# Two-layer decoder on one core: input norms moved ahead of the bitnet weight scaling, score tiles preset on ScalarE, attention tables loaded from the sync queue

## The chip, the core and the metric

The kernel runs as one program on one core of a Trainium2 chip. The metric is the device time in microseconds from launch to end; lower is better. The engines are called as the profile calls them: PE (TensorE matmuls), PEld (its weight loads), DVE (VectorE), ACT (ScalarE), POOL (GpSimd) and SP (SyncE, which here only issues transfers).

## The reference, cut to what matters

Sixteen sequences of 128 tokens with 128 channels pass through two decoder layers, each with a self-attention part, a cross-attention part and a feed-forward part, and each part sits behind a plain layer norm. Only the pieces that the change touches are shown in code.

```python
x = x + _L0_attn_ref(_layernorm(x), ...)            # 4 encoder layers with linear attention
x = x + _L0_xattn_ref(_layernorm(x), ctx, ctx, mask, ...)
x = x + _L0_ffn_ref(_layernorm(x), w1, conv_w, conv_b, w2)   # bitnet layer
x = x + _L1_attn_ref(_layernorm(x), ...)            # top-64 attention
x = x + _L1_xattn_ref(_layernorm(x), ctx, ctx, ...) # channel attention
x = x + _L1_ffn_ref(_layernorm(x), Wg, Wu, Wd)      # 8 experts

# _L0_attn_ref begins:
x = math.sqrt(d) * x_in + _sinusoidal_pos_emb(t, d)[None]
h = _layernorm(x, ln1_s, ln1_b); q, k, v = h @ Wq + bq, h @ Wk + bk, h @ Wv + bv
# _L0_xattn_ref:
scores = jnp.where(mask == 0, NEG, q k^T / sqrt(8)); weights = softmax(scores)
# _L0_ffn_ref, for both weights:
def weight_quant(w):
    scale = 1.0 / jnp.clip(jnp.mean(jnp.abs(w)), 1e-05)
    return jnp.clip(jnp.round(w * scale), -1, 1) / scale
```

## The kernel before, in words

The sixteen sequences are cut into two halves of eight, and a half into two slots (s = 0, 1) of four sequences. A tile such as `xin[s]`, `h[s]` or `xs_of[half][s]` holds the four sequences of a slot, tokens on the partitions. The program is written out by hand for each engine; the order of the work is the order of that text, and semaphores join the engines.

The first half goes through the four encoder layers in a loop (`encode_half`, PE line 1708, DVE line 2386), then through cross attention and the bitnet feed-forward (`cross_and_forward(0)`). After that the second half's encoder steps are woven into the top-64 attention of the first half (`beside_encoder`, which is made of `merged_turn(b)` for b from -1 to 9), then `cross_and_forward(1)`, and then the rest of the top-64 attention with the experts.

The opening, ahead of the loop: POOL starts the load of the raw bitnet weights (`wc_raw`, which lies in the buffer `far0`), sets constant tiles, issues eight loads of attention tables on its own queue (lines 625 to 629) and then serves the norms. SP loads the two slots of x, then `ident`, `consts`, `pos`, `maskt`, `rowf` (semaphore `consts_in`, 80 when all five are in), and then the first layer's weights. DVE waits for `consts_in` at 80, quantizes the bitnet weights (lines 2215 to 2230: absolute sums, a cross-partition sum by one PE matmul at line 1704, scaling, rounding, clipping to `wcq`), and only then runs the norm of the inputs.

A layer norm of a slot is four `bn_stats` and four `bn_aggr` on DVE (lines 1878 and 1883), two small operations on POOL that make `rstd` (lines 637 and 639), and four `tensor_scalar` on DVE that write `h` (line 1890). The inputs are normed (LN_IN), scaled and given the position table (line 2247), and normed again (LN_A, the first norm of the encoder layer). PE transposes that `h` (line 1268), ACT copies it to `hT` (line 932), PE projects it (lines 1720 and 1722), and DVE adds the bias rows to keys and values (`kk`, `vv`, lines 2392 and 2393): the first `kk` is where the loop's steady work on DVE begins. These are counted in units of half a slot.

The masked scores of the cross attention are built by a predicated copy of PSUM into a tile `S` that must hold NEG beforehand. `S` has three buffers. POOL fills them with three memsets (`preset_scores`, line 828) twice: in the opening behind the first input norms, and in turn 9 of `beside_encoder`, behind the `rstd` of the cross-attention norm of the second half.

## Time and profile before

| | |
|---|---|
| three runs, median (lowest to highest) | 1449.4 us (1447.85 to 1454.92) |
| the profiled execution's own time | 1452.7 us |
| its span, first to last instruction | 1450.9 us |
| busy: PE, PEld, DVE, ACT, POOL | 1053.8, 695.7, 998.0, 671.1, 491.9 us |
| mean granted PE clock | 0.819 of full |

The busy times are sums over a program whose stages have different limits, so none of them says what bounds a given stage. The chain of work that ended last, followed back from the end, says which engine was waited for; the timeline of a stretch says what stood there. Both are in the rows further down. Times in a timeline count from the span's start.

### The profile page before, as it was taken

How to read it: one execution, taken by the hardware profiler on the slowest of the kernel's cores; microseconds unless marked ns; L12 is line 12 of the kernel's file. 1: busy time of each engine (PE TensorE's matmuls, PEld its weight loads, DVE VectorE, ACT ScalarE, POOL GpSimd, SP SyncE). 2: the span in 40 equal slices, each digit the busy share in tenths (PEclk: the TensorE clock that was granted, in tenths of full speed). 3: DMA queues.
4: the chain of work that ended last, by engine and by line, in shares of the span. 5: the costliest groups of instructions: out<-in, count | busy, mean ns of one | idle time of the engine just before them, and what ended most of it. 6: DMA issues, size and time to landing. Idle time of an engine off the chain costs nothing.

```text
span 1450.9 us, 17892 instructions
## 1 busy us (share of the span) xinstructions
PE 1053.8 (73%) x5079; PEld 695.7 (48%) x5082; DVE 998.0 (69%) x3100; ACT 671.1 (46%) x1767; POOL 491.9 (34%) x474
## 2 busy tenths in 40 slices
PE   2877775655476818777676669868899883888999
PEld 1766652323344515554454334433344462666887
DVE  5666657878637778778887886753776858765332
ACT  1443436733156526666423654325776653533322
POOL 5233235601335404444524730043343423331100
PEclk9898976765677767888655889989998986899999
DMA  3000110000000000000001001201111120223344
GB/s 124 21 18 29 29 41 9 1 0 1 0 10 21 12 3 17 14 17 9 1 1 51 1 1 37 66 22 47 52 45 45 48 73 15 67 77 92 113 135 123
DMA packets 41106, 53.88 MB, mean 37 GB/s; under 512 B 6112, under 2 KB 20080, under 8 KB 41008
## 3 DMA queue, kind: packets, MB, share of 16 engines
q1 hardware_dynamic: 40336, 50.80, 11.5%
q0 software_dynamic: 672, 1.98, 0.4%
q8 instruction: 37, 0.61, 0.2%
q14 instruction: 61, 0.50, 0.1%
HBM read 51.71 MB, written 1.05 MB: 36 GB/s over the span
## 4 chain that ended last, share of the span: by engine, by line
PE 49%; DVE 28%; ACT 7%; POOL 7%; issue 7%; DVEq 1%; DMA 0%; another core or an unknown queue 0%; SPq 0%; POOLq 0%; ACTq 0%
PE psum L1679 7%; PE psum L1690 6%; PE psum L1665 6%; PE psum L1450 2%; PE psum L1426 2%; PE psum L1757 2%; PE psum L1268 2%; PE psum L1346 2%; PE psum L1544 2%; DVE h L1890 2%; PE psum L1408 2%; PE psum L1764 2%; POOL Wk L680 2%; PE psum L1498 2%; ACT far L995 2%
## 5 line engine op out<-in xcount | busy, mean ns | idle before, releaser
L2188 DVE TENSOR_TENSOR big<-psum,qe 128x512 f32<-128x512 f32 x106 | 72.8, 687 | 154.7 <-PE psum L1690 75.4
L1144 ACT ACTIVATE qe<-psum 128x512 f32<-128x512 f32 x106 | 62.3, 596 | 124.4 <-PE psum L1679 120.3
L1665 PE MATMUL psum<-big,wexp 128*128 128x256 f32 (+1 forms) x340 | 115.8, 455 | 0.0
L995 ACT ACTIVATE far<-far,half_far,fmul 128x128 bf16<-128x128 bf16 x256 | 102.9, 488 | 22.7 <-DVE hit L1963 22.7
L637 POOL TENSOR_SCALAR veps<-mv 128x4 f32<-128x4 f32 x34 | 8.4, 246 | 294.6 <-DVE mv L1883 294.6
L1976 DVE MAX8 near<-Wk 128x8 f32<-128x128 f32 x512 | 103.0, 275 | 0.0
L1268 PE MATMUL psum<-ident,h 128*128 128x128 f32 x172 | 37.9, 347 | 78.4 <-DVE h L1890 53.3
L735 POOL TENSOR_TENSOR Wk<-Wk,far 128x1024 f32<-128x1024 f32 x32 | 68.2, 2136 | 67.9 <-ACT far L995 67.9
L1890 DVE TENSOR_SCALAR h<-xs,mv,rstd 128x128 f32<-128x128 f32 x128 | 57.9, 553 | 41.1 <-POOL rstd L639 37.9
L1665 PEld LDWEIGHTS psum<-big,wexp 128*128 128x128 f32 x340 | 69.0, 203 | 30.1 <-issue 21.9
L1346 PE MATMUL psum<-ident,Wk 128*128 128x128 f32 x256 | 48.0, 355 | 47.1 <-POOL Wk L680 44.2
L1690 PE MATMUL psum<-xin,wexp 128*128 128x512 f32 x128 | 70.4, 633 | 15.1 <-DVE far L2188 9.9
L973 ACT ACTIVATE S<-psum,tiny 128x1024 f32<-128x1024 f32 x32 | 35.7, 1114 | 92.3 <-PE psum L1408 92.3
L1679 PE MATMUL psum<-xin,wexp 128*128 128x512 f32 x128 | 76.0, 679 | 2.5 <-DVE vaug L2599 1.6
L985 ACT ACTIVATE far<-S 128x128 bf16<-128x128 f32 x256 | 75.0, 296 | 0.3
L726 POOL TENSOR_TENSOR Wk<-S,ngr 128x2048 f32<-128x2048 f32 x16 | 58.1, 3630 | 39.1 <-DVE hit L1963 39.1
L1346 PEld LDWEIGHTS psum<-ident,Wk 128*128 128x128 f32 x256 | 38.0, 182 | 69.0 <-POOL Wk L680 42.5
L1268 PEld LDWEIGHTS psum<-ident,h 128*128 128x128 f32 x172 | 23.5, 171 | 97.9 <-DVE h L1890 47.5
L757 POOL TENSOR_SCALAR nparts<-nmax 128x16 bf16<-128x16 f32 x16 | 5.2, 326 | 189.2 <-DVE nmax L2060 189.2
L1986 DVE MATCH_REPLACE8 Wk<-near,Wk 128x128 f32<-128x128 f32 x256 | 67.1, 273 | 0.0
L1426 PE MATMUL psum<-ctxT,kT 32*128 32x512 f32 x128 | 49.0, 848 | 23.4 <-DVEq L2054 22.2
L948 ACT ACTIVATE Wk<-S,nsm 128x128 f32<-128x128 f32 x128 | 49.5, 389 | 11.9 <-DVE nsm L2480 11.9
(343 smaller groups left out, 2915.0 us busy)
## 6 DMA issues: line engine op xcount, KB each, us to landing
wexp<-in_mg SPq DMA_DIRECT2D x48, 256.0 KB, 2.7
wexp<-in_mu SPq DMA_DIRECT2D x48, 256.0 KB, 3.0
wexp<-in_md SPq DMA_DIRECT2D x48, 256.0 KB, 3.0
w<-in_aw SPq DMA_DIRECT2D x8, 256.0 KB, 2.9
w<-in_w2a SPq DMA_DIRECT2D x8, 256.0 KB, 2.6
wqkv<-in_aw SPq DMA_DIRECT2D x8, 192.0 KB, 2.2
ctxt<-in_ctx SPq DMA_DIRECT2D x5, 256.0 KB, 4.6
xin<-in_x SPq DMA_DIRECT2D x4, 256.0 KB, 3.0
```

The lines of the kernel that those rows point to most:

```text
L735: pool.tensor_tensor(Wk[t][:, heads, :], Wk[t][:, heads, :], far[t][:, heads, :], ALU.subtract).then_inc(z_ready, 1)
L985: ins = act.activation(far[n % 2][:, hd, :], S[n % 3][:, hd, :], ACT.Sign, accum_out=cnt[n % 2][:, hd:hd + 1])
L995: ins = act.activation(far[t][:, hd, :], far[t][:, hd, :], ACT.Identity, bias=half_far[:, 0:1], scale=fmul[t][:, hd:hd + 1])
L1268: mm = pe.transpose(dst[:, b * P:(b + 1) * P], src[:, b, :], eye)
L1346: mm = pe.transpose(bank(4 + g % 2)[:, j * P:(j + 1) * P], E[a % 2][:, 4 * g + j, :], ident[:, :])
L1426: pe.matmul(bank(j), kT_of[g // 2][g % 2][rows, c * P:(c + 1) * P], qblk[a % 2][rows, :, :].rearrange("p i q -> p (i q)"), start=True, sto ...
L1665: mm = pe.matmul(bank(4)[:, 0:w], wd[l % 2][:, c + j, :], hid_of[k >= EARLY][k % CH][:, j * w:(j + 1) * w], start=first and j == 0, stop=l ...
L1679: mm = pe.matmul(bank(5 + k % 2)[:, j * w:(j + 1) * w], wg[l % 2][:, (c + j) * P:(c + j + 1) * P], hTm[g], start=True, stop=True)
L1690: mm = pe.matmul(bank(U_BANK[k])[:, j * w:(j + 1) * w], wu[l % 2][:, (c + j) * P:(c + j + 1) * P], hTm[g], start=True, stop=True)
L1890: ins = dve.tensor_scalar(h[s][:, b, :], src[:, b, :], mv[s][:, b, 0:1], rstd[s][:, b:b + 1], ALU.subtract, ALU.mult)
L1976: ins = dve.max(near[:, hd, rank:rank + 8], Wk[t][:, hd, :])
L2188: dve.tensor_tensor(hid_of[k >= EARLY][k % CH], bank(U_BANK[k]), sg_of[k >= EARLY][k % 2], ALU.mult).then_inc(hu_done, 1)
```

## The change

In words: DVE opens with the statistics of the inputs; the absolute sums of the bitnet weights are made on ACT (`Abs` with an accumulated output, its elementwise result thrown into `big0`); their scaling and rounding go in two pieces between and behind the norms of the first encoder layer. The score tiles are filled by ACT (Identity of a zero tile with NEG as bias) instead of POOL, in the opening as ACT's first work and in turns 8 and 9 of `beside_encoder`. The eight loads of attention tables and the loads of `maskt` and `rowf` go to the end of SP's opening list; `consts_in` is waited for at 48 (`ident`, `pos`, `consts`), and the attention tables' semaphore at 128 instead of 96. DVE waits once for all three presets. The first embedding is written out as `first_embedding`, with the two slots interleaved differently.

```diff
@@ SP, opening
-for dst, src in ((ident..), (consts..), (pos..), (maskt[:, :], mask)):
+for dst, src in ((ident..), (pos..), (consts..)):
     sp.dma_start(dst, src).then_inc(consts_in, 16)
-sp.dma_start(rowf[:, :], arow[L:L + 1, 0:2 * P].to_broadcast([P, 2 * P])).then_inc(consts_in, 16)
 for load in (load_qkv, load_out, load_up, load_down):
     load(0)
 for s in SL:
     load_ctx(s, s * G)
+sp.dma_start(maskt[:, :], mask).then_inc(attw_in, 16)
+sp.dma_start(rowf[:, :], ...).then_inc(attw_in, 16)
+for i in range(2):
+    sp.dma_start(watt[i]..), sp.dma_start(catt[i]..), sp.dma_start(ratt[i]..)   # attw_in
+sp.dma_start(rowe..), sp.dma_start(cole..)                                      # ew_in
@@ POOL
+pool.memset(masked[:, :], NEG)
-for i in range(2):
-    pool.dma_start(watt[i]..), pool.dma_start(catt[i]..), pool.dma_start(ratt[i]..)
-pool.dma_start(rowe..), pool.dma_start(cole..)
 pool.wait_ge(preset, 1)
-pool.wait_ge(consts_in, 80)
 for s in SL:
     ln_rsqrt(s, LN_IN)
+pool.wait_ge(consts_in, 48)
-def preset_scores():
-    for t in range(3):
-        pool.memset(S[t][:, :, :], NEG).then_inc(s_preset, 1)
@@ POOL, beside_encoder, turn NB + 1
-    pool.wait_ge(drop_done, NB)
-    preset_scores()
@@ POOL, ahead of encode_half
-preset_scores()
@@ ACT
+def preset_scores(t):
+    act.activation(S[t][:, :, :], zeros[:, :].unsqueeze(1).to_broadcast([P, H, P]), ACT.Identity, bias=masked[:, 0:1]).then_inc(s_preset, 1)
 act.wait_ge(preset, 1)
+for t in range(3):
+    preset_scores(t)
+act.wait_ge(cw_in, 32)
+for k in range(2):
+    act.activation(big[0][:, k, :], wc_raw[:, k, :], ACT.Abs, accum_out=wsum[:, k:k + 1]).then_inc(wq_sem, 1)
@@ ACT, beside_encoder
 for b in range(-1, NB + 2):
+    if b == NB + 1:
+        act.wait_ge(drop_done, NB)
+        preset_scores((NB - 1) % 3)
     merged_turn(b)
...
     if b == NB:
         beside(4)
+        for n in (NB - 3, NB - 2):
+            act.wait_ge(drop_done, n + 1)
+            preset_scores(n % 3)
         context_keys(1)
@@ PE
-pe.wait_ge(consts_in, 80)
+pe.wait_ge(consts_in, 48)
@@ DVE
-dve.wait_ge(consts_in, 80)
-dve.wait_ge(preset, 1)
-dve.tensor_copy(identb..); dve.tensor_scalar(neg_big..)
-dve.wait_ge(cw_in, 32)
-for k in range(2):
-    dve.tensor_reduce(wsum[:, k:k + 1], wc_raw[:, k, :], AX.X, ALU.add, apply_absolute_value=True).then_inc(wq_sem, 1)
-...                       # wscale, wrs, scaling, rounding, clipping
 for s in SL:
     dve.wait_ge(x_in[s], 16)
     layer_norm(s, LN_IN, xin[s])
-for s in SL:
-    normalize(s, LN_IN, xin[s])
+def first_embedding():
+    def embedded(s):
+        normalize(s, LN_IN, xin[s])
+        if s == 0:
+            dve.wait_ge(consts_in, 48)
+        dve.wait_ge(ln_h, both(s, LN_IN + 1))
+        dve.scalar_tensor_tensor(xs_of[0][s].., h[s].., float(np.sqrt(P)), pos.., ALU.mult, ALU.add).then_inc(x_upd, 2)
+    embedded(0)
+    dve.wait_ge(x_upd, both(0, LN_A))
+    layer_norm(0, LN_A)
+    embedded(1)
+    normalize(0, LN_A)
+    dve.wait_ge(x_upd, both(1, LN_A))
+    layer_norm(1, LN_A)
+    weights_scaled()      # waits for the PE sum; wscale, wrs, scaling of both weights
+    normalize(1, LN_A)
+    weights_rounded()     # rounding, identb, neg_big, clipping to wcq
@@ DVE, cross_and_forward
-if b < 3:
-    dve.wait_ge(s_preset, hf * 3 + (b + 1))
+if b == 0:
+    dve.wait_ge(s_preset, hf * 3 + 3)
```

DVE's first instructions in the program before, from behind two small operations on `ident` up to the first norm written to `h`, read as follows (`xs0_0` is the first half's slot 0 of x, `far0` holds the raw bitnet weights).

```order
L2219 TENSOR_REDUCE wsum<-far0 128x1 x2
L2221 TENSOR_SCALAR wscale<-psum 128x2
L2223 RECIPROCAL wrs<-wscale 128x2
L2226 TENSOR_SCALAR far0<-far0,wrs 128x512 x2
L2228 TENSOR_SCALAR far0<-far0 128x1024
L2230 TENSOR_SCALAR wcq<-far0 128x1024
L1878 BN_STATS stats0<-xin0 128x6 x4
L1883 BN_AGGR mv0<-stats0 128x2 x4
L1878 BN_STATS stats1<-xin1 128x6 x4
L1883 BN_AGGR mv1<-stats1 128x2 x4
L1890 TENSOR_SCALAR h0<-xin0,mv0,rstd0 128x128 x4
L1890 TENSOR_SCALAR h1<-xin1,mv1,rstd1 128x128 x4
```

The same engine in the changed program, from the second slot's embedding to the entry of the encoder loop; the four statistics groups of the inputs, slot 0's first `h`, its embedding and its second statistics stand ahead of these rows.

```order
L2253 SCALAR_TENSOR_TENSOR xs0_1<-h1,pos 128x512
L1901 TENSOR_SCALAR h0<-xs0_0,mv0,rstd0 128x128 x4
L1889 BN_STATS stats1<-xs0_1 128x6 x4
L1894 BN_AGGR mv1<-stats1 128x2 x4
L2230 TENSOR_SCALAR wscale<-psum 128x2
L2232 RECIPROCAL wrs<-wscale 128x2
L2235 TENSOR_SCALAR far0<-far0,wrs 128x512 x2
L1901 TENSOR_SCALAR h1<-xs0_1,mv1,rstd1 128x128 x4
L2239 TENSOR_SCALAR far0<-far0 128x1024
L2240 CAST identb<-ident 128x128
L2241 TENSOR_SCALAR neg_big<-ident 128x128
L2243 TENSOR_SCALAR wcq<-far0 128x1024
```

The weight work moved from ahead of the first norm to both sides of the last one, and the two reductions that made `wsum` are gone from this engine.

On ACT, between turn 8 and turn 9 of `beside_encoder`, the program before has these rows (`at`, `kT1` and `hT` carry the cross attention's context, keys and queries of the second half; line 1004 is the softmax exponential of the top-64 attention).

```order
L1135 ACTIVATE se2<-se2 128x256
L1197 COPY at0<-psum 128x512
L1197 COPY at1<-psum 128x512
L1200 ACTIVATE kT1_0<-psum,catt0 128x512
L1200 ACTIVATE kT1_1<-psum,catt0 128x512
L1004 ACTIVATE wexp<-psum 128x1024
L927 COPY hT0<-psum 128x512
```

The changed program has there:

```order
L1138 ACTIVATE se2<-se2 128x256
L1156 ACTIVATE S2<-zeros,masked 128x2048
L1156 ACTIVATE S0<-zeros,masked 128x2048
L1209 COPY at0<-psum 128x512
L1209 COPY at1<-psum 128x512
L1212 ACTIVATE kT1_0<-psum,catt0 128x512
L1212 ACTIVATE kT1_1<-psum,catt0 128x512
L1156 ACTIVATE S1<-zeros,masked 128x2048
L1001 ACTIVATE wexp<-psum 128x1024
L924 COPY hT0<-psum 128x512
```

Two presets stand ahead of the copies of the context, and the third between the keys and the exponential.

## Rows read from the trace of the kernel before

**Rows 1.** The page's chain that ended last, by engine.

```profile
PE 49%; DVE 28%; ACT 7%; POOL 7%; issue 7%; DVEq 1%; DMA 0%; another core or an unknown queue 0%; SPq 0%; POOLq 0%; ACTq 0%
```

**Rows 2.** The chain's pieces in the opening: start us, us, what.

```profile
1.24 0.49 SPq L483
...
2.79 0.43 SPq L534
...
3.74 4.89 DMA rowf<-in_arow
```

**Rows 3.** DMA issues of the opening: size, median us from issue to landing.

```profile
xin<-in_x SPq DMA_DIRECT2D x1, 256.0 KB, 4.5
...
pos<-in_pos SPq DMA_DIRECT2D x1, 64.0 KB, 4.4
```

**Rows 4.** Timeline of DVE in the opening: start us, us, engine, line.

```profile
8.66 0.23 DVE L2215 CAST identb<-ident 128x128 bf16<-128x128 f32 x1 [8.66 <-DMA rowf<-in_arow]
...
10.95 0.16 DVE L2221 TENSOR_SCALAR wscale<-psum 128x2 f32<-128x2 f32 x1 [0.74 <-PE psum L1704]
...
12.26 0.69 DVE L2228 TENSOR_SCALAR far<-far 128x1024 f32<-128x1024 f32 x1
...
13.60 0.87 DVE L1878 BATCH_NORM_STATS2 stats<-xin 128x6 f32<-128x128 f32 x4
...
16.76 1.12 DVE L1890 TENSOR_SCALAR h<-xin,mv,rstd 128x128 f32<-128x128 f32 x4 [0.49 <-POOL rstd L639]
...
18.10 5.86 DVE L1890 TENSOR_SCALAR h<-xin,mv,rstd 128x128 f32<-128x128 f32 x4 [0.23 <-POOL rstd L639]
...
23.88 0.68 DVE L2247 SCALAR_TENSOR_TENSOR xs<-h,pos 128x512 f32<-128x512 f32 x1
...
25.62 0.38 DVE L1883 BATCH_NORM_AGGREGATE mv<-stats 128x2 f32<-128x6 f32 x4
...
27.66 1.11 DVE L1890 TENSOR_SCALAR h<-xs,mv,rstd 128x128 f32<-128x128 f32 x4 [1.67 <-POOL rstd L639]
...
33.77 0.42 DVE L2392 TENSOR_TENSOR kk<-psum,rowkv 128x256 f32<-128x256 f32 x1
```

**Rows 5.** POOL: its last constant tile, and line 828, all instructions.

```profile
4.03 0.22 POOL L623 MEMSET zeros<- 128x128 bf16 x1
...
L828 POOL MEMSET S<- x6: 1805/1806/1807, 18.0 to 762.5; 128x2048 f32 x6
```

**Rows 6.** Timeline of PE in the opening.

```profile
28.32 1.20 PE L1268 MATMUL psum<-ident,h 128*128 128x128 f32 x4 [17.41 <-DVE h L1890]
...
35.15 1.13 PE L1720 MATMUL psum<-wqkv,hT 128*128 128x256 f32 x4 [0.80 <-ACT hT L932]
```

**Rows 7.** ACT instruction groups by form: busy us, mean ns of one, idle before.

```profile
L985 ACT ACTIVATE far<-S 128x128 bf16<-128x128 f32 x256 | 75.0, 296 | 0.3
...
L951 ACT ACTIVATE Wk<-S 128x1024 f32<-128x1024 f32 x16 | 16.7, 1043 | 0.0
...
L1044 ACT ACTIVATE ke<-kk 128x512 f32<-128x512 f32 x8 | 5.0, 628 | 0.0
```

**Rows 8.** Timelines of DVE, PE and ACT around turn 9.

```profile
747.52 0.59 ACT L1197 COPY at<-psum 128x512 f32<-128x512 f32 x1 [8.72 <-PE psum L1268]
...
757.44 1.02 ACT L1004 ACTIVATE wexp<-psum 128x1024 f32<-128x1024 f32 x1 [3.81 <-PE psum L1433]
...
759.11 5.86 DVE L1890 TENSOR_SCALAR h<-xs,mv,rstd 128x128 f32<-128x128 f32 x4 [0.69 <-POOL rstd L639]
...
764.58 1.03 PE L1433 MATMUL psum<-neg_big,drop 128*128 128x128 bf16 x8
...
767.64 1.26 DVE L2440 TENSOR_TENSOR vv<-psum,ratt 128x512 f32<-128x512 f32 x2
...
768.40 1.08 PE L1268 MATMUL psum<-ident,h 128*128 128x128 f32 x4 [2.79 <-issue]
```

**Rows 9.** PE by windows: stretch, its us, busy (count), granted clock, DMA.

```profile
760.00:780.00 20.00, 15.36 (x58) 0.50 0.00 1
...
0.00:1450.00 1450.00, 1053.75 (x5079) 0.82 0.12 37
```

More of the change, by code:

```diff
@@ L321, in decoder @@
         tiny = sb("tiny", [P, 1])
+        masked = sb("masked", [P, 1])
         neg_big = sb("neg_big", [P, P], BF16)
@@ L532, in _ @@
                 load_x(s, s * G)
-            for dst, src in ((ident[:, :], ident_d), (consts[:, :], const_d), (pos[:, :], pos_d), (maskt[:, :], mask)):
+            for dst, src in ((ident[:, :], ident_d), (pos[:, :], pos_d), (consts[:, :], const_d)):
                 sp.dma_start(dst, src).then_inc(consts_in, 16)
-            sp.dma_start(rowf[:, :], arow[L:L + 1, 0:2 * P].to_broadcast([P, 2 * P])).then_inc(consts_in, 16)
             for load in (load_qkv, load_out, load_up, load_down):
@@ L539, in _ @@
                 load_ctx(s, s * G)
+            sp.dma_start(maskt[:, :], mask).then_inc(attw_in, 16)
+            sp.dma_start(rowf[:, :], arow[L:L + 1, 0:2 * P].to_broadcast([P, 2 * P])).then_inc(attw_in, 16)
+            for i in range(2):
+                sp.dma_start(watt[i][:, :], (bw, dw)[i]).then_inc(attw_in, 16)
+                sp.dma_start(catt[i][:, :], (bcol, dcol)[i]).then_inc(attw_in, 16)
+                sp.dma_start(ratt[i][:, :], (brow, drow)[i].to_broadcast([P, 2 * P])).then_inc(attw_in, 16)
+            sp.dma_start(rowe[:, :, :].rearrange("p a c -> p (a c)"), erow.to_broadcast([P, 10 * P])).then_inc(ew_in, 16)
+            sp.dma_start(cole[:, :], ecol).then_inc(ew_in, 16)
             for hf in range(1):
@@ L2210, in act_scales @@
                 dve.tensor_scalar(asc[s][:, :], asc[s][:, :], 127.0, None, ALU.mult).then_inc(c_step[s], 1)
-            dve.wait_ge(consts_in, 80)
-            dve.wait_ge(preset, 1)
-            dve.tensor_copy(identb[:, :], ident[:, :])
-            dve.tensor_scalar(neg_big[:, :], ident[:, :], -BIG, None, ALU.mult)
-            dve.wait_ge(cw_in, 32)
-            for k in range(2):
-                dve.tensor_reduce(wsum[:, k:k + 1], wc_raw[:, k, :], AX.X, ALU.add, apply_absolute_value=True).then_inc(wq_sem, 1)
-            dve.wait_ge(wsum_mm, 1)
-            dve.tensor_scalar(wscale[:, :], bank(7)[:, 0:2], 1.0 / (P * FH), 1e-5, ALU.mult, ALU.max).then_inc(wq_sem, 1)
-            dve.wait_ge(wq_sem, 3)
-            dve.reciprocal(wrs[:, :], wscale[:, :]).then_inc(wq_sem, 1)
-            dve.wait_ge(wq_sem, 4)
-            for k in range(2):
-                dve.tensor_scalar(wc_raw[:, k, :], wc_raw[:, k, :], wrs[:, k:k + 1], MAGIC, ALU.mult, ALU.add).then_inc(wq_sem, 1)
-            dve.wait_ge(wq_sem, 6)
-            dve.tensor_scalar(wc_raw[:, :, :], wc_raw[:, :, :], MAGIC, 1.0, ALU.subtract, ALU.min).then_inc(wq_sem, 1)
-            dve.wait_ge(wq_sem, 7)
-            dve.tensor_scalar(wcq[:, :, :], wc_raw[:, :, :], -1.0, None, ALU.max).then_inc(wq_sem, 1)
             for s in SL:
@@ L2235, in _, with weights_scaled, weights_rounded @@
                 layer_norm(s, LN_IN, xin[s])
-            for s in SL:
-                normalize(s, LN_IN, xin[s])
+            def weights_scaled():
+                dve.wait_ge(wsum_mm, 1)
+                dve.tensor_scalar(wscale[:, :], bank(7)[:, 0:2], 1.0 / (P * FH), 1e-5, ALU.mult, ALU.max).then_inc(wq_sem, 1)
+                dve.wait_ge(wq_sem, 3)
+                dve.reciprocal(wrs[:, :], wscale[:, :]).then_inc(wq_sem, 1)
+                dve.wait_ge(wq_sem, 4)
+                for k in range(2):
+                    dve.tensor_scalar(wc_raw[:, k, :], wc_raw[:, k, :], wrs[:, k:k + 1], MAGIC, ALU.mult, ALU.add).then_inc(wq_sem, 1)
+            def weights_rounded():
+                dve.wait_ge(wq_sem, 6)
+                dve.tensor_scalar(wc_raw[:, :, :], wc_raw[:, :, :], MAGIC, 1.0, ALU.subtract, ALU.min).then_inc(wq_sem, 1)
+                dve.tensor_copy(identb[:, :], ident[:, :])
+                dve.tensor_scalar(neg_big[:, :], ident[:, :], -BIG, None, ALU.mult)
+                dve.wait_ge(wq_sem, 7)
+                dve.tensor_scalar(wcq[:, :, :], wc_raw[:, :, :], -1.0, None, ALU.max).then_inc(wq_sem, 1)
+            def first_embedding():
[4 more added lines that the diff above has]
+                    dve.wait_ge(ln_h, both(s, LN_IN + 1))
+                    dve.scalar_tensor_tensor(xs_of[0][s][:, :, :], h[s][:, :, :], float(np.sqrt(P)), pos[:, :].unsqueeze(1).to_broadcast([P, G, P]),
+                                             ALU.mult, ALU.add).then_inc(x_upd, 2)
+                embedded(0)
[8 more added lines that the diff above has]
+                weights_rounded()
             def embed(hf):
@@ L2612, in cross_and_forward @@
                         normalize(s, n0 + (NLN + LN_IN), xin[s])
-            embed(0)
+            first_embedding()
             encode_half()
```

13 lines of the change are left out of this document (4 added, 9 removed).

## The prediction, made before the changed kernel ran

> **What bounds the kernel now.** I read the page's chain that ended last first. PE holds 49% of it and DVE 28% [rows 1]: no single engine bounds the program, so a saving counts only where the chain passes. The change touches two places, the opening and turn 9 of the interleaved encoder, so I read the chain and the timelines of these two.
>
> In the opening PE stands still until 28.32 us, for 17.41 us of it waiting for `h` from DVE [rows 6]. DVE is the engine that everybody waits for. It does nothing until 8.66 us, when the last of the five constant loads, `rowf`, has landed: the chain has a piece of 4.89 us for that transfer [rows 2, 4]. Then it works on the bitnet weights until 13.60, when the statistics of the inputs begin [rows 4]. The inputs had been there long before: the second slot of x was issued at 1.24 and took 4.5 us, so it lay ready at 5.74 [rows 2, 3].
>
> There is a third loss in the same stretch. Four `tensor_scalar` of one norm take 1.12 us at 16.76, but the next four, the same instruction on the other slot, take 5.86 us at 18.10 [rows 4]. They lie beside POOL's three memsets of the score tiles, of 1.806 us each, the first of which starts at 18.0 [rows 5]. The same picture returns near 759: four such instructions take 5.86 us while the other three of the six memsets run, whose last starts at 762.5 [rows 5, 8].
>
> **The opening, step by step.** What is new is DVE's order. I price each step from its own row and let it start when the one before it ends or its input is there. A statistics pass (stats and aggregate) is the time from the end of the embedding (23.88 + 0.68 = 24.56) to the end of the aggregates (25.62 + 0.38 = 26.00), so 1.44 us; from there to the norm that uses it, through POOL's two small operations, it is 27.66 - 26.00 = 1.66 us [rows 4].
>
> Slot 1 of x lands at 5.74; its pass ends at 7.2, slot 0's having run before it. Norm of slot 0, 1.12: 8.3. Embedding, 0.68: 9.0; it needs `pos`, which landed at 2.79 + 4.4 = 7.2 even with more transfers ahead [rows 2, 3]. Pass of slot 0, 1.44: 10.4. Norm and embedding of slot 1, 1.12 + 0.68: 12.2. Norm of slot 0 for the encoder, whose `rstd` is there at 10.4 + 1.66 = 12.1, 1.11: 13.4. Pass of slot 1: 14.8. Scaling of the weights, from 10.95 to 12.26 in the old timeline, 1.31: 16.1. Norm of slot 1, `rstd` there at 14.8 + 1.66 = 16.5, 1.11: 17.6. Rounding and clipping, 13.60 - 12.26 = 1.34, and two casts of at most 0.23 each: 19.4. So the first `kk` comes at 19.4 instead of 33.77 [rows 4]: **14.4 us earlier**. Of these, 5.86 - 1.12 = 4.7 are the memsets' share.
>
> What lies beside it. PE must first do the little sum of the weights, and that now waits for ACT: three presets and two Abs passes behind POOL's last constant tile, which ends at 4.03 + 0.22 = 4.25 [rows 5]. A preset of 2048 elements is an operation that the trace does not show. The nearest row is the longest plain SBUF-to-SBUF activation, 1043 ns for 1024 elements; against 628 ns for 512 that is 0.81 ns an element, so 1.04 + 0.83 = 1.87 us, and at most 2.09 as two of them [rows 7]. The far upper bound is sixteen instructions of 128 elements, 16 x 296 ns = 4.7 us; the lower bound is that of an operation hidden altogether, zero [rows 7]. I take 2.0, since this one has a bias column and one instruction pays its start only once. ACT is then through at 4.25 + 6.0 = 10.3. The Abs passes are 128x512, 0.63 each and something for the accumulated output, 1.5 together: 11.8. PE has the sum well before 13, and DVE asks for it at 14.8. It costs nothing; the slack is about 2.5 us, or 0.8 a preset.
>
> The Trainium skill, "ScalarE: Activation LUTs", section "What ACT_TABLE_LOAD costs", gives an activation with a bias column as about 1990 ns at 2048 elements, with 93 ns of overlap between neighbours. By it three presets take 5.8 us and the sum stays the same; no row of the trace before has such an instruction.
>
> PE's own work fits too. In the old order the third unit's projections are done at 35.15 + 1.13 = 36.28, 2.5 us after the second `h` was complete and `kk` began at 33.77 [rows 4, 6]. From 17.6 that gives 20.1, and DVE reaches the third unit only some 2.5 us behind its first `kk`, at 21.9. So DVE's weight rounding is what is late next, by 1.8 us, and that is in the sum.
>
> The loads. SP's first three transfers keep their places, the layer weights move two issues forward, and the eight table loads leave POOL's queue for the end of SP's. They feed the cross attention, which comes after all four encoder layers of the first half: cost nothing. If SP's queue were slow in taking them, the next layer's weights would wait behind them; but these are only asked for when the first layer's attention is done. POOL loses eight issues that nobody waited for.
>
> **Turn 9.** Without the memsets the four `tensor_scalar` at 759.11 take 1.1 us, so DVE is 4.7 us earlier from there. PE does not follow by as much. It finished its batch at 764.58 + 1.03 = 765.61 and then stood 2.79 us until 768.40 [rows 8], although the `h` it transposes was ready at 764.97. In the code it also waits for the first `vv` of the cross values (`pv_done`), whose pair of instructions began at 767.64, so the first ended at 768.3 [rows 8]. With DVE 4.7 us earlier that is 763.6, before PE is free at 765.61. So the whole gap goes: **2.8 us**, and PE's own batch is next.
>
> On ACT the presets of `S2` and `S0` (4 us) fall in the 8.72 us in which it stood idle ahead of 747.52, and that of `S1` in the 3.81 us ahead of 757.44 [rows 8]. If that cover were gone the third would delay the exponential by 2.0 us.
>
> **Sum.** 14.4 + 2.8 = 17.2 us. The profiled execution took 1452.7, which gives 1435.5; the median of the three runs is 1449.4, 3.3 below it, and gives 1432. I forecast **1432 us**.
>
> **The rivals.**
> *Only the opening pays.* At turn 9 another wait replaces the removed one, or the gain meets work further on that is not earlier (the experts' loads, a POOL step). For it: DVE moves 4.7 and PE only 2.8, so there are joints at which gains shrink. Against it: PE is on the chain there, and what it does next is its own. 1449.4 - 14.4 = 1435. Chance 0.14.
> *The presets are slow.* If an activation that reads a repeated zero tile goes at the short instructions' rate, 4.7 us each [rows 7], ACT has the absolute sums at 4.25 + 14.2 + 1.5 = 20.0. PE cannot transpose before 20.6; DVE, at 14.8, waits for the sum until 20.6, and `kk` comes at 20.6 + 1.3 + 1.1 + 1.8 = 24.8. Gain 9 in the opening, 11.8 in all: 1438. It decides from 2.8 us a preset on. Chance 0.07.
> *The clock rises.* Around turn 9 PE has 0.50 of its clock, the 1.2 GHz level, with 15.36 us of work in 20 [rows 9]. A closed gap there could bring the upper level sooner; half of 15.36 is 7.7, and if two thirds of it are on the path, 5 us more are gained: 1427. The Trainium skill, "TensorE: Matmul & The Clock Gate", section "HAM oscillation — how this bites in real kernels", says that idle gaps of PE bring the lower clock; no row says yet that this gap does. Chance 0.08.
> *The clock takes part back.* Every later stage starts some 15 us earlier against whatever else sets the clock, and stretches at 0.50 may fall elsewhere. 6 us back: 1438. Chance 0.07.
> *Slower than before, by the clock.* PE's part of the chain is 0.49 x 1450.9 = 711 us at a mean of 0.82 [rows 1, 9]. To lose the 17.2 and 7.2 more, 711 x (0.82 / c - 1) must be 24.4, so c = 0.793. Above 1456.6 from there on. Against it: no engine gets more idle time. Chance 0.03; with c between 0.80 and 0.81 the result is no change, 1442 to 1456, with other absorptions 0.05.
>
> **How the numbers follow.** The forecast, both gains to within 5 us, has the remaining 0.56. Its bounds, the rival with the opening alone, the slow presets and the clock either way lie between 1426 and 1440; that holds a little over 0.8. What a measurement here tells from no change is 0.5%, 7.2 us. Faster by more than that, below 1442.2: 0.92. Within it: 0.05. Slower: 0.03.
>
> **What would show it.** In the changed trace: DVE's first statistics before 6 us instead of at 13.60; the four `tensor_scalar` of both norms at 1.1 us; ACT's presets at 2.0 us each and the absolute sums by 12; PE's first transposes near 13; the first `kk` near 19.4; around turn 9 no 5.86 us group, and no gap of 2.8 us ahead of PE's second set of transposes. Wrong would be: `tensor_scalar` still at 5.86 (another partner than the memsets), a transfer that lands later than x or `pos` did, the sum of the weights later than 15 us, or a mean clock that differs by 0.01 or more, which alone is worth 9 us.

## The result and the profile after

| | before | after |
|---|---|---|
| median of the executions (us) | 1450.77 (1447.85 to 1454.92, 4 runs) | 1432.62 (1430.56 to 1438.47, 4 runs) |
| ratio, 95% interval | | 0.9882 (0.9847 to 0.9917) |
| profiled execution, its span (us) | 1452.7, 1450.9 | 1434.47, 1432.3 |
| its mean granted clock | 0.819 | 0.822 |

The change makes the kernel 18 us faster. The forecast was 1432, in a range of 1426 to 1440. The same kernel, timed again with others (again_after below), gave 1430.94 against 1453.09, ratio 0.9873 (0.9831 to 0.9915). One execution of weights_late below took 1582.62 us at a mean granted clock of 0.667, and is left out of its figures.

The chain that ended last, from the page of after, answers to [rows 1]; its pieces in the opening answer to [rows 2] (start us, us, what):

```profile
PE 49%; DVE 28%; ACT 8%; issue 7%; POOL 6%; DVEq 1%; DMA 0%; another core or an unknown queue 0%; SPq 0%; POOLq 0%; ACTq 0%
```

```profile
2.32 0.43 SPq L535
...
2.79 5.45 DMA consts<-in_const
```

The chain still begins with a load, but it is that of `consts`, and it holds the embedding up for only 0.17 us, as DVE's timeline of after says (to be held against [rows 4]):

```profile
3.57 0.87 DVE L1889 BATCH_NORM_STATS2 stats<-xin 128x6 f32<-128x128 f32 x4 [3.57 <-DMA xin<-in_x]
...
7.09 1.09 DVE L1901 TENSOR_SCALAR h<-xin,mv,rstd 128x128 f32<-128x128 f32 x4
8.34 0.69 DVE L2253 SCALAR_TENSOR_TENSOR xs<-h,pos 128x512 f32<-128x512 f32 x1 [0.17 <-DMA consts<-in_const]
...
14.89 0.88 DVE L2235 TENSOR_SCALAR far<-far,wrs 128x512 f32<-128x512 f32 x2
...
16.31 1.12 DVE L1901 TENSOR_SCALAR h<-xs,mv,rstd 128x128 f32<-128x128 f32 x4 [0.53 <-POOL rstd L641]
...
18.82 0.42 DVE L2421 TENSOR_TENSOR kk<-psum,rowkv 128x256 f32<-128x256 f32 x1
```

ACT in the opening, then the group of all presets, which is the row that [rows 7] did not have (count: shortest/middle/longest ns):

```profile
4.32 5.79 ACT L1156 ACTIVATE S<-zeros,masked 128x2048 f32<-128x2048 bf16 x3 [2.30 <-POOL zeros L632]
...
11.15 0.19 ACT L1163 ACTIVATION_READ_ACCUMULATOR big<-far 128x1 f32 x1
```

```profile
L1156 ACT ACTIVATE S<-zeros,masked x6: 1986/1991/2001, 4.3 to 735.6; 128x2048 f32<-128x2048 bf16 x6
```

PE in the opening, against [rows 6]:

```profile
12.85 1.20 PE L1280 MATMUL psum<-ident,h 128*128 128x128 f32 x4 [0.82 <-DVE h L1901]
...
20.19 1.13 PE L1731 MATMUL psum<-wqkv,hT 128*128 128x256 f32 x4 [1.17 <-ACT hT L929]
```

The timelines of DVE, PE and ACT of after around turn 9, against [rows 8]:

```profile
720.79 3.88 ACT L1156 ACTIVATE S<-zeros,masked 128x2048 f32<-128x2048 bf16 x2
...
735.62 1.99 ACT L1156 ACTIVATE S<-zeros,masked 128x2048 f32<-128x2048 bf16 x1
...
740.87 1.12 DVE L1901 TENSOR_SCALAR h<-xs,mv,rstd 128x128 f32<-128x128 f32 x4 [0.69 <-POOL rstd L641]
...
740.33 0.63 PE L1280 MATMUL psum<-ident,h 128*128 128x128 f32 x4 [0.83 <-DVE h L1901]
...
744.02 0.62 PE L1445 MATMUL psum<-neg_big,drop 128*128 128x128 bf16 x8
745.42 0.63 PE L1280 MATMUL psum<-ident,h 128*128 128x128 f32 x4 [0.77 <-issue]
746.78 1.13 PE L1295 MATMUL psum<-hT,watt 128*128 128x512 f32 x2 [0.73 <-ACT hT L924]
747.74 3.69 PE L1462 MATMUL psum<-vaug,wexp 128*128 128x10 f32 x32
```

Everything on the list of what would show the forecast right is there: DVE's first statistics at 3.57, none of the norms' `tensor_scalar` groups in the opening and in turn 9 longer than 1.12, presets of 1.99 us, sums through by 11.34, PE's first transposes at 12.85, the first `kk` at 18.82. At turn 9 PE stands 0.77 us instead of 2.79. But something else moved there too. Eight matmuls on `neg_big` take 0.62 us instead of 1.03 [rows 8]. In the kernel before, the first transposes and the two groups behind the second ones are these:

```profile
758.57 0.84 PE L1268 MATMUL psum<-ident,h 128*128 128x128 f32 x4 [1.16 <-DVE h L1890]
...
770.22 2.08 PE L1283 MATMUL psum<-hT,watt 128*128 128x512 f32 x2 [0.73 <-ACT hT L927]
772.08 6.84 PE L1450 MATMUL psum<-vaug,wexp 128*128 128x10 f32 x32
```

They take 0.63, 1.13 and 3.69 us after. That is the upper level of the clock, 2.4 GHz, instead of the lower one, 1.2 GHz.

PE's matmuls come in the same order in all of these kernels. So the start of the k-th matmul in two traces can be subtracted, and each stretch shows what it gains or gives back. Most traces hold 5,079 matmuls; those of presets_only, t9_pool, open_pool and tables_pool hold three more, whose records the others lack, and the table counts without these three. The table is worked out from the traces: the time of the k-th matmul in the first trace of before, then how much earlier (-) it starts in the other traces.

```
matmul  before |  again_  again_  |  after  again_ | presets_  t9_    open_ | xb_
                  before  before_2          after      only    pool   pool  | late
   14     32.5    -0.1     +0.6    -15.0   -14.9      -3.6    -15.0  -11.5   -15.1
  900    254.8    -0.1     -1.8    -14.7   -17.0      -8.0    -17.1  -14.4   -27.6
 1050    297.6    -0.1     -4.7    -17.5   -19.9      -7.6    -19.9  -14.4   -27.6
 2550    755.5    -0.1     -5.2    -17.9   -20.4      -6.7    -20.3  -14.4   -24.3
 2640    785.4    -0.1     -5.2    -27.4   -29.8      -9.7    -21.4  -24.0   -33.9
 3300    987.5    -0.1     -5.2    -24.9   -27.3     -10.1    -20.3  -24.6   -34.5
 3600   1097.3    -0.2     -5.2    -21.2   -23.7     -10.1    -16.8  -21.1   -31.0
 4500   1326.9    -0.1     -5.2    -18.5   -23.7      -7.4    -15.3  -17.9   -28.1
  end   1447.9    -0.1     -5.2    -18.7   -23.7      -7.5    -13.6  -17.9   -28.4
```

In the column of after, the opening brings 15.0 and keeps it (14.7 at 254.8). Another 2.7 come between 254.8 and 297.6. Turn 9 brings 9.5, and from there to 1326.9 some 9 are given back. PE by windows shows whose gain and loss that is (stretch, its us, PE busy and count, granted clock, DMA). The stretches are set so that nearly the same matmuls lie in them, first in before and then in after:

```profile
755.00:785.00 30.00, 22.84 (x95) 0.56 0.03 7
812.00:903.00 91.00, 65.20 (x286) 0.88 0.05 15
903.00:1097.00 194.00, 163.42 (x601) 0.91 0.14 43
```

```profile
737.00:758.00 21.00, 16.10 (x98) 0.84 0.07 19
784.00:877.00 93.00, 69.18 (x282) 0.82 0.05 15
877.00:1076.00 199.00, 167.90 (x603) 0.90 0.13 42
```

The same work keeps PE busy for 6.7 us less in the first stretch, and for 4.0 and 4.5 us more in the other two. The granted clock is higher in the first and lower in the others.

### The profile page after: what moved, and what is told of

The parts are those of the page before. It is cut to its first block, busy times and chain, and to the rows that moved or that the text cites. A ratio compares the mean times of both kernels' runs of the same rounds, so it can differ in the third digit from the quotient of the medians.

```text
span 1432.3 us, 17890 instructions
## 1 busy us (share of the span) xinstructions
PE 1051.4 (73%) x5079; PEld 694.3 (48%) x5082; DVE 987.0 (69%) x3098; ACT 679.6 (47%) x1774; POOL 477.7 (33%) x461
## 4 chain that ended last, share of the span: by engine, by line
PE 49%; DVE 28%; ACT 8%; issue 7%; POOL 6%; DVEq 1%; DMA 0%; another core or an unknown queue 0%; SPq 0%; POOLq 0%; ACTq 0%
PE psum L1691 7%; PE psum L1702 6%; PE psum L1677 6%; PE psum L1768 2%; PE psum L1438 2%; PE psum L1462 2%; PE psum L1280 2%; PE psum L1556 2%; PE psum L1420 2%; PE psum L1775 2%; DVE h L1901 2%; PE psum L1358 2%; PE psum L1510 2%; POOL Wk L682 2%; ACT far L992 2%
## 5 line engine op out<-in xcount | busy, mean ns | idle before, releaser
L1901 DVE TENSOR_SCALAR h<-xs,mv,rstd 128x128 f32<-128x128 f32 x128 | 53.1, 477 | 38.4 <-POOL rstd L641 35.1
```

Source lines behind the costliest of these rows:

```text
L1901: ins = dve.tensor_scalar(h[s][:, b, :], src[:, b, :], mv[s][:, b, 0:1], rstd[s][:, b:b + 1], ALU.subtract, ALU.mult)
```

## The experiments

**t9_pool: turn 9 undone alone.** The opening stays as changed. POOL presets the tiles at turn 9, and ACT's presets there are taken out.

```diff
+            def preset_scores():
+                for t in range(3):
+                    pool.memset(S[t][:, :, :], NEG).then_inc(s_preset, 1)
...
                     if b == NB + 1:
+                        pool.wait_ge(drop_done, NB)
+                        preset_scores()
...
```

> The changed kernel with the three presets of turn 9 back on POOL as memsets; the opening as changed. Theory A (the memsets hold up DVE, and PE waits for DVE there): the four tensor_scalar beside them take 5.9 us again, and PE's second set of transposes in turn 9 comes 2.8 us later than in the changed kernel at the low clock, up to 4.7 us at the high one, where PE waits less on itself. Time 3 to 5 us over the changed kernel. Rival B (what the changed kernel gained there came from the clock alone, which rose at turn 9): tensor_scalar slow, but PE's later start of the scores is the same within 1 us when the clock is the same, and the time is the changed kernel's within 1 us.

Measured: 1440.26 (1437.81 to 1443.35, 6 runs), ratio 0.9911 (0.9886 to 0.9936) to a before of 1453.62. DVE's, POOL's and PE's timelines at turn 9:

```profile
738.36 5.29 POOL L832 MEMSET S<- 128x2048 f32 x3
...
738.44 5.86 DVE L1901 TENSOR_SCALAR h<-xs,mv,rstd 128x128 f32<-128x128 f32 x4 [0.68 <-POOL rstd L641]
...
737.90 0.63 PE L1280 MATMUL psum<-ident,h 128*128 128x128 f32 x4 [0.83 <-DVE h L1901]
...
747.73 1.09 PE L1280 MATMUL psum<-ident,h 128*128 128x128 f32 x4 [5.52 <-DVE vv L2469]
749.55 2.08 PE L1295 MATMUL psum<-hT,watt 128*128 128x512 f32 x2 [0.73 <-ACT hT L930]
```

PE stands 5.5 us, and behind that its matmuls are at the lower level again. In the table the kernel is level with again_after up to matmul 2550 and 8.4 us behind it at 2640. So taking the memsets out of turn 9 is worth 8 us here, more than the 3 to 5 expected; the wait makes 5.52 - 0.77 = 4.7 of it, and the slower matmuls the rest.

The first transposes, ahead of that wait, are still at the upper level (0.63 us, behind a stand of 0.83). So it wasn't the closed gap that kept the clock up there: the kernel before has the lower level at this place, and so has presets_only. The stand ahead of the first transposes is 0.83 to 0.85 us in all ten traces with the new opening, and 1.14 to 1.17 in the three of before and that of presets_only. The third of a microsecond comes from DVE, which begins the group of instructions ahead of it sooner, in before and then in after:

```profile
750.23 0.69 DVE L2444 TENSOR_TENSOR h<-h,rowf 128x512 f32<-128x512 f32 x1 [1.41 <-issue]
```

```profile
732.00 0.69 DVE L2473 TENSOR_TENSOR h<-h,rowf 128x512 f32<-128x512 f32 x1 [1.08 <-issue]
```

"issue" is time in which DVE waited for nothing that the profile shows. It is 1.41 in the four traces with the old opening and 1.08 to 1.09 in the ten with the new one. No experiment moved it alone, so that it tips the clock is argued, not shown.

**open_pool: the opening's memsets undone alone.** POOL presets the tiles behind the two input norms.

```diff
...
+            preset_scores()
             encode_half()
...
             act.wait_ge(preset, 1)
-            for t in range(3):
-                preset_scores(t)
```

> The changed kernel with the opening's presets back on POOL as memsets behind the rstd of the inputs; ACT does only the absolute sums there. Theory A: the memsets fill POOL from 8.9 to 14.2 us. DVE's norm of slot 1 at 10.4 is held until about 14.2, and the rstd of the first encoder norm, asked for at 10.5, comes only at 15.5 instead of 12.2. First kk at 22.5 instead of 18.8, time 3.5 to 4 us over the changed kernel. Rival B (order of DVE alone made the gain, the memsets cost nothing): first kk within 0.5 us of 18.8.

Measured: 1433.12 (1429.85 to 1434.86, 5 runs), ratio 0.9851 (0.9824 to 0.9878). The first `kk` comes at 22.20, 3.4 us later, because one norm meets the memsets:

```profile
10.49 4.36 DVE L1904 TENSOR_SCALAR h<-xin,mv,rstd 128x128 f32<-128x128 f32 x4
```

The local step is as expected, and the time is not: it can't be told from that of after.

**tables_pool: the table loads back on POOL.** The eight transfers of attention tables are issued by POOL ahead of its first norm; the rest stays as changed.

```diff
             pool.memset(zeros[:, :], 0.0).then_inc(preset, 1)
+            for i in range(2):
+                pool.dma_start(watt[i][:, :], (bw, dw)[i]).then_inc(attw_in, 16)
+                pool.dma_start(catt[i][:, :], (bcol, dcol)[i]).then_inc(attw_in, 16)
+                pool.dma_start(ratt[i][:, :], (brow, drow)[i].to_broadcast([P, 2 * P])).then_inc(attw_in, 16)
...
```

> The changed kernel with the eight loads of attention tables issued by POOL again, behind its constant tiles, as in the kernel before; maskt and rowf stay at the end of SP's list. The prediction held that nobody waited for these issues. Theory A (true only in the old order): eight issues of 0.52 us keep POOL from 4.3 until 8.5 us, so the rstd of the inputs' slot 0 is ready at 9.8 instead of 6.6, DVE's first norm starts at 9.8 instead of 7.1 and the first kk comes at 21.5, 2.7 us later; time 2 to 3 us over the changed kernel. Rival B (the prediction's own reading, nobody waits): first kk within 0.3 us of 18.8, time the same.

Measured: 1433.21 (1431.59 to 1435.85, 4 runs), ratio 0.9857 (0.9825 to 0.9889). POOL begins its two small operations only at 8.54, when its last issue is done, and DVE waits:

```profile
7.89 0.53 POOL L632 DMA_DIRECT2D cole<-in_ecol  x1
...
9.95 1.12 DVE L1901 TENSOR_SCALAR h<-xin,mv,rstd 128x128 f32<-128x128 f32 x4 [2.90 <-POOL rstd L641]
```

The first `kk` comes at 21.68, 2.9 us later than after. Moving the loads is a part of the opening's gain, then. The time again doesn't show it. By the traces both kernels are still 3.2 to 3.5 us behind the trace of after at matmul 150 (65 us) and within 0.4 of it at 750 (196 us). But they are 2.3 to 2.6 behind again_after there, so this catching up is no larger than the scatter between two executions of one kernel. Whether the 3 us are paid up to turn 9 stays open. Behind it something else covers them: both traces of after lose 2.5 to 2.6 us between 2640 and 3300, and open_pool and tables_pool gain 0.6 there.

**presets_only: ACT's presets alone, in the old order.**

```diff
...
-            preset_scores()
             encode_half()
...
             act.wait_ge(preset, 1)
+            for t in range(3):
+                preset_scores(t)
...
```

> The kernel before with nothing changed but the presets: all six on ACT, in the opening and in turns 8 and 9. Theory A: both groups of tensor_scalar at 1.1 us instead of 5.9; first kk at 29.0 instead of 33.8; PE's transposes in turn 9 another 2.8 us earlier or more. Time 7 to 9 us under the kernel before, so the order of the opening is worth the other 10. Rival B (in the old order the removed stall is filled by the next wait, POOL's rstd): first kk not before 31, time 3 to 5 us under the kernel before.

Measured: 1445.19 (1440.62 to 1445.92, 6 runs), ratio 0.9931 (0.9905 to 0.9957): 8.4 us less than before. The first `kk` comes at 29.96, 3.8 us earlier; it would be 4.7, but `rowf` landed at 9.60 instead of 8.66. At turn 9, where ACT has the presets too, the table gives 3.0 us, close to the predicted 2.8. PE's timeline there:

```profile
751.86 0.84 PE L1275 MATMUL psum<-ident,h 128*128 128x128 f32 x4 [1.17 <-DVE h L1897]
...
757.88 1.03 PE L1440 MATMUL psum<-neg_big,drop 128*128 128x128 bf16 x8
758.70 1.06 PE L1275 MATMUL psum<-ident,h 128*128 128x128 f32 x4
```

The gap ahead of the second transposes is gone whole, yet PE had come to the lower level at 751.86, with the first transposes, after 1.17 us of idling, and stays there. So this kernel shows the step by itself, without the clock's share.

**again_after and again_before: how much is scatter.** Both are unaltered kernels.

> The changed kernel again, unaltered, timed beside the three below on one chip, so that they can be compared with it and not with a kernel before that ran elsewhere. Theory A (each local step is worth its time, the granted clock adds or takes a few us): 1432 to 1436 us, so that open_pool (1433.1) and tables_pool (1433.2) are level with it although their first kk is 2.8 to 3.3 us later. Theory B (those two lost their 3 us on the path all the way and only ran on a chip or at a moment that favoured them): this one comes out near 1430 us, ratio to before 0.983 or lower. The profile should show the first kk again within 0.5 us of 18.8, the second transposes of turn 9 without a gap of more than 1 us, and the matmuls behind them at 1.1 us for four.

> The kernel before, unaltered, for a second trace of it, to see how far two executions of one kernel part by the granted clock alone. Theory A (the 8 us that the changed kernel gave back between 900 and 1330 us are scatter of the clock: the first trace of before had the clock at 0.91 there by chance): this trace's clock over 1000 to 1200 us is nearer 0.85 to 0.88, and its matmuls there are 3 us or more later against the first trace. Theory B (they belong to the change: the experts run slower when what is ahead of them ended sooner): the clock there is 0.90 or more again and the two traces agree within 2 us at every matmul. Turn 9: PE's second transposes again 2.8 us after the first, and the matmuls behind them at 2.1 us for four.

> The kernel before a third time, as again_before: by theory A the clock over 1000 to 1200 us scatters between traces by 0.02 or more, by theory B the three agree within 0.01.

Measured: again_after 1430.94 (1426.31 to 1440.81, 6 runs), its profiled execution 1429.46; the two of before 1452.68 and 1447.53. In the table, again_before agrees with the first trace to 0.2 us at every matmul. again_before_2 runs 5.2 us ahead, and has all of that by 432 us; 2.9 of them fall between 254.8 and 297.6, where after gained its 2.7. From there on all three are parallel; their clock from 1000 to 1200 us is 0.91, 0.91 and 0.90. So the 2.7 us are scatter. What was given back behind turn 9 is so only for the smaller part. Up to matmul 3600 both traces of after give back the same 6.1 to 6.2 us, and no trace of before does. Of these, 3.6 fall between 3300 and 3600, in all ten traces with the new opening; the other 2.5 to 2.6 fall before 3300, in both traces of after and in joints_late, but not in open_pool, tables_pool, weights_late and xb_late. The further 2.7 up to 4500 are in the first trace of after and not in again_after; ten of the eleven traces of changed kernels lose 1.5 to 3.5 us there. Theory A of these expectations falls for the larger part, and holds at most for these 2.7.

**xb_late: another meeting of POOL and DVE taken away.** POOL's two additions of the attention's output bias wait for the last unit's queries.

```diff
                     pool.wait_ge(wo_in, i * 32 + 32)
+                    pool.wait_ge(q_pos, nth_unit(UNITS - 1, i + 1))
                     for s in SL:
                         pool.tensor_tensor(xb[s][:, :, :], xs[s][:, :, :], bc(rowo[:, :]), ALU.add).then_inc(xbo_done, 1)
```

> In every layer GpSimd's tensor_tensor adds of the bias row wait until the last unit's normalised input has been written, instead of running beside VectorE's residual adds; nothing else changes. In the changed kernel these residual adds of VectorE take 1.47 and 1.49 us beside GpSimd and 0.53 and 0.41 us elsewhere. Theory A (an elementwise GpSimd instruction holds up a VectorE instruction that meets it): the two groups fall to about 0.5 and 0.4 us, some 2 us a layer, 4 layers, so 6 to 8 us less: 1425 to 1428 us against 1433 of the changed kernel. Rival (the VectorE adds are slow for another reason, a PSUM read for example): the groups stay at 1.5 us and the time at 1433. Second rival (they fall, but PE's clock takes the gain back): groups at 0.5 us and 1430 to 1433 us.

(The two DVE groups form the positive keys and queries; to call them residual additions was a slip of the expectation.) Measured: 1419.99 (1418.5 to 1424.69, 5 runs), ratio 0.9779 (0.9745 to 0.9814), 11 us below again_after in the same comparison. It beats both kernels. The first layer in after, then in xb_late:

```profile
24.32 2.72 POOL L883 TENSOR_TENSOR xb<-xs,rowo 128x512 f32<-128x512 f32 x2
...
24.46 1.47 DVE L1909 SCALAR_TENSOR_TENSOR big<-ke,big 128x256 f32<-128x256 f32 x1
25.85 1.49 DVE L1914 SCALAR_TENSOR_TENSOR qT<-qe,qT 128x256 f32<-128x256 f32 x1
```

```profile
24.14 0.42 DVE L1910 SCALAR_TENSOR_TENSOR big<-ke,big 128x256 f32<-128x256 f32 x1
24.49 0.42 DVE L1915 SCALAR_TENSOR_TENSOR qT<-qe,qT 128x256 f32<-128x256 f32 x1
...
25.25 0.41 DVE L2433 TENSOR_TENSOR kvs<-psum,consts 128x256 f32<-128x256 f32 x1
...
25.06 2.50 POOL L884 TENSOR_TENSOR xb<-xs,rowo 128x512 f32<-128x512 f32 x2 [1.02 <-DVE qT L1915]
```

Theory A holds at the rows, 1.47 + 1.49 - 0.42 - 0.42 = 2.1 us a layer and 8.5 in four; POOL's additions start 0.7 us later and hold up nobody. In the table the lead over again_after is 10.6 us at 254.8; the 2 above the sum I put down to the clock, and by the end of the two profiled executions 4.7 remain. The profiled one of xb_late was the slowest of its five. The medians say 11, more than the 6 to 8 expected.

**joints_late: and one more, at the joint to the cross attention.** On top of xb_late, POOL spreads the first two rows before it makes the second slot's `rstd`, and the third row and the bias additions come behind that.

```diff
-                for b in range(2):
-                    spread(b)
+                spread(0)
+                spread(1)
                 if hf == 0:
+                    ln_rsqrt(1, LN_B)
                     pool.wait_ge(attw_in, 16 * 8)
+                spread(2)
...
-                spread(2)
...
```

> xb_late, and in addition at the joint of self and cross attention GpSimd first gives the 1/std of the first two units and only then spreads the third row; the bias adds come behind it. In the changed kernel one VectorE normalisation at 199.1 us takes 4.50 us beside GpSimd's tensor_tensor adds, where its like take 1.1. Theory A: that instruction comes down to 1.1 to 1.5 us and the copy of the following scores at 204.1 us comes about 1.8 us earlier, so 1 to 2 us below xb_late. Rival (the gain goes into the wait for the score copy on ScalarE): the instruction falls but the score copy stays at 204, and the time is that of xb_late within 0.5 us.

Measured: 1420.72 (1413.21 to 1433.97, 6 runs), ratio 0.9785 (0.9738 to 0.9832). The norm came down from 4.50 to 1.11 us, but the norm of the other slot, which now meets the two spreads, went up from 1.11 to 2.57, and PE makes DVE wait 1.16 us behind it. So the copy of the first scores came from 191.27 to 190.16, 1.1 us. The time can't be told from xb_late's.

**weights_late: is the weight rounding late next?** Scaling and rounding move behind the self attention, to an idle stretch of DVE ahead of their first use.

```diff
+                    if hf == 0 and b == 3:
+                        weights_rounded()
...
-                weights_rounded()
```

> The scaling and rounding of the ternary weights moves from in front of the first kk to a place behind the last unit's statistics, where VectorE idles 6.3 us. The prediction said that the rounding would be late next, by 1.8 us, once the norms open the program. Theory A: the first kk comes at 16.4 to 17.5 instead of 18.8 us, but the third unit's matmuls wait for ScalarE's copy of their transposes, so only 0.5 us or so reaches the third kk (21.4) and the time is 1432 to 1433.5, the same as the changed kernel within the measurement. Rival (all of the rounding was on the path): the third kk at 19 us and the time about 2.4 us lower. Slower by 1 to 3 us if the moved work lands in front of something that waits for VectorE.

Measured: 1432.44 (1429.85 to 1434.71, 5 runs), ratio 0.9863 (0.9828 to 0.9898), which can't be told from again_after. The first `kk` is at 17.01 instead of 18.66, the third only at 20.85 instead of 21.21, since DVE now waits 0.81 us for PE's third unit:

```profile
20.85 0.42 DVE L2420 TENSOR_TENSOR kk<-psum,rowkv 128x256 f32<-128x256 f32 x1 [0.81 <-PE psum L1731]
```

**memset_waits and memset_pieces: how the hold works.** Both start from t9_pool. One waits for the end of each memset; the other cuts each in four.

```diff
                     pool.memset(S[t][:, :, :], NEG).then_inc(s_preset, 1)
+                    pool.wait_ge(s_preset, 3 + t + 1)
```

```diff
-                    pool.memset(S[t][:, :, :], NEG).then_inc(s_preset, 1)
+                    for g in range(0, H, 4):
+                        ins = pool.memset(S[t][:, g:g + 4, :], NEG)
+                    ins.then_inc(s_preset, 1)
```

> t9_pool again (all three score tiles preset by GpSimd at turn 9), with GpSimd waiting for the completion of each memset before it issues the next. In t9_pool one VectorE tensor_scalar that met the three memsets at 738.4 took 5.86 us, about their whole 5.29 us. Theory A (VectorE is shut out as long as GpSimd's memsets follow without a break, and gets in at a break): the instruction takes 2 to 2.6 us, and PE's second transposes come some 3 to 3.7 us after where they were in t9_pool's own order, near 744 rather than 747.7. Rival (the instruction's four parts each lose to a memset whatever lies between, or VectorE's access is slowed all the time while GpSimd has any memset left): it stays above 5 us.

> t9_pool again with each of the three memsets cut into four (twelve of 128x512 in a row, no wait between them). Theory A (the hold lasts as long as the memsets follow without a break, whatever their size): the VectorE tensor_scalar that meets them stays at 5 to 6 us. Rival (it lasts one memset, and t9_pool's long one was only unlucky in meeting three of its parts): it takes under 3.5 us, since a memset now takes about 0.5 us. The time of this kernel is near t9_pool's 1440 us by the first, near 1436 by the second, which one look can't settle; the row decides.

Measured: 1442.74 and 1443.73, one execution each. The four instructions of the norm by themselves, with the waits, and then with the pieces:

```profile
L1902 DVE TENSOR_SCALAR h<-xs,mv,rstd x4: 1609/1760/1900, 741.8 to 743.9; 128x128 f32<-128x128 f32 x4
```

```profile
L1903 DVE TENSOR_SCALAR h<-xs,mv,rstd x4: 329/2894/5646, 743.1 to 749.0; 128x128 f32<-128x128 f32 x4
```

In t9_pool the same line reads:

```profile
L1901 DVE TENSOR_SCALAR h<-xs,mv,rstd x4: 327/2712/5285, 738.4 to 744.0; 128x128 f32<-128x128 f32 x4
```

With twelve short memsets in a row (524 to 525 ns each) the group took 6.22 us, and its first instruction 5.646. So the length of a memset doesn't matter, the unbroken row does: the rival of memset_pieces falls. With breaks the hold ends at each, but two of the four instructions get in and the next two meet the next memset: 3.76 us, neither the 2 to 2.6 of theory A nor the over 5 of the rival. Theory A had the mechanism, and counted one memset too few. PE stood 3.46 us instead of 5.52 ahead of the second transposes, and was at the lower level behind that too.

## Why the prediction was right

**The opening, 14.4 us.** Measured at the first `kk`, 33.77 - 18.82 = 14.95; on PE, 15.0, of which 14.7 are still there at 255 us. Down to the scaling of the weights, through at 14.89 + 0.88 = 15.77 instead of 16.1, every step lies within 0.4 us of its forecast, and the rounding overlapped a little more than priced.

**"Of these, 4.7 are the memsets' share."** Right as a mechanism. In the old order their removal gave 3.8 (0.9 lost to a later `rowf`); in the new order their return costs 3.4, since a norm met only 4.36 us of them.

**The preset, 2.0 us.** Measured 1.99. Here the Trainium skill, "ScalarE: Activation LUTs", section "What ACT_TABLE_LOAD costs", with its 1990 ns, was nearer than the reach from neighbouring rows (1.87); this trace agrees with it.

**"Weight rounding is late next, by 1.8 us."** This step failed, without harm to the sum. It looked at when DVE reaches the third unit and took PE's projections as done at 20.1. They began at 20.19, after 1.17 us of waiting for ACT's copy, and ended at 21.32; the third `kk` began at 21.36. weights_late showed it: 1.65 us at the first `kk` and 0.36 at the third.

**"POOL loses eight issues that nobody waited for."** Right in the old order and wrong in the new one: tables_pool puts 2.90 us of DVE's wait there. I had priced the removal in an order in which the norms came late. In the sum this did no harm either, since the sum was built on the new order with the loads gone.

**Turn 9, 2.8 us.** presets_only has it alone: 3.0. In the changed kernel turn 9 brought 9.5. The rest is the rival *the clock rises*, which I gave 0.08 and 5 us: PE stayed at the upper level from its first transposes until 751 us, and its matmuls there took about half their time. The rival had the mechanism only in part. It let the closed gap of 2.79 us bring the level; the level was there before that gap, with the new opening and its shorter stand of 0.83 us, and the closed gap kept it. The opening alone gains 1.1 us at turn 9 (t9_pool, where the wait swallows the rest), the presets alone 3.0 (presets_only), both together 9.5. All of open_pool, tables_pool, again_after and weights_late have both, and 9.5 to 9.6 us.

**The clock takes part back** had 0.07 and 6 us, and it happened too: some 9 us between 785 and 1327. The rows of one place, before and after, for the same matmuls:

```profile
1055.99 1.02 PE L1665 MATMUL psum<-big,wexp 128*128 128x512 f32 x2
```

```profile
1031.81 1.91 PE L1677 MATMUL psum<-big,wexp 128*128 128x512 f32 x2
```

There is no wait in it. Between matmuls 3300 and 3600 all ten traces with the new opening lose 3.6 us, and presets_only and the three traces of before lose none. The first 0.3 of it come before the clock differs. DVE aggregates a norm without a break in before, and with one in after:

```profile
991.18 0.38 DVE L2113 BATCH_NORM_AGGREGATE mv<-stats 128x2 f32<-128x6 f32 x4
```

```profile
966.33 0.18 DVE L2124 BATCH_NORM_AGGREGATE mv<-stats 128x2 f32<-128x6 f32 x1
966.71 0.31 DVE L2124 BATCH_NORM_AGGREGATE mv<-stats 128x2 f32<-128x6 f32 x3 [0.20 <-issue]
```

The break is in all ten traces with the new opening and in no other, and PE then waits 3.37 us for `h` instead of 3.06. The remaining 3.3 us are matmuls at the lower level, at two places behind it. The prediction took these rivals as alternatives of which one decides. Both came and cancelled: 9.5 - 2.8 = 6.7 us more at turn 9 and 2.7 of scatter at 255 to 298, against 8.9 given back, of which 6.2 in both traces of after. So the mechanisms were right, and that the profiled executions differ by 18.2 where the sum said 17.2 is partly luck. "A mean clock that differs by 0.01" was a poor test: 0.819 and 0.822 hide a stretch that rose from 0.56 to 0.84 and one that fell from 0.88 to 0.82.

**What stays open:** whether the moved fractions of "issue" on DVE, 0.33 us at turn 9 and 0.31 in the experts, are what tips the clock there. How much earlier the experts start doesn't seem to set it: the kernels that lose the 3.6 us reach matmul 3300 between 16 and 36 us earlier than before, and lose the same. No experiment moved such a fraction alone.

## What to carry to other kernels

When one instruction takes five times as long as its twin, look at what the other engine that shares its memory path is doing, on every row of the kind and not only where the time is large: the same kind of meeting as the memsets', with POOL's ordinary additions, was worth as much as turn 9, and one wait removed it. Price what a queue loses or gains in the order that the change makes, not in the old one. Where PE is between its two clock levels, subtract the start times of the same matmuls in two traces (match them by name first, since some records can be missing), and take two traces of each kernel: that separates a step's own gain, what the clock adds or takes, and scatter; a mean clock over the program does not.

## What the runs showed of the hardware

- A row of GpSimd memsets without a break holds a VectorE `tensor_scalar` for the whole row: 5285 ns beside three of 1805 ns, 5646 ns beside twelve of 525 ns, 1802 ns for the first where GpSimd waits between them. The Trainium skill, "SBUF — State Buffer", section "Who interferes with whom", has the pair of ports as a lock that the first holds for its instruction while the other blocks. The trace agrees with the lock; that it isn't handed over between two instructions that follow at once, only the runs show.
- The hold depends on the form. In memset_waits the third memset runs from 745.5 to 747.3, and beside it a VectorE `scalar_tensor_tensor` from PSUM took 0.67 us and a `tensor_tensor` of two SBUF tiles 0.69, their usual times. Beside GpSimd's `tensor_tensor`, which reads SBUF, a `scalar_tensor_tensor` of two SBUF tiles took 1.47 instead of 0.42 (after), and a `tensor_tensor` with one input in PSUM its usual 0.41 (xb_late, at 25.25). The same section of the Trainium skill says that an instruction with two SBUF inputs meets only GpSimd instructions that read SBUF; the trace agrees.
- Two executions of one kernel can part early (5.2 us by 432 us) and then stay parallel to within 0.5 us at every matmul for 1000 us: the matmuls take the same level of the clock at the same places. So the 3.6 us between matmuls 3300 and 3600, which all ten traces with the new opening lose and the other four do not, are hardly scatter.
